# Batch 1's row maxima beside batch 0's scores: three banks, the free row groups, and an earlier place in the step

## What is computed

```python
scores = jnp.einsum('bshd,bthd->bhst', q, k) / jnp.sqrt(HEAD_DIM)
scores = jnp.where(causal, scores, -jnp.inf)
probs = jax.nn.softmax(scores, axis=-1)
out = jnp.einsum('bhst,bthd->bshd', probs, v)
```

## Time and profile before

| | us |
|---|---|
| median of 3 runs | 650.36 |
| the runs | 649.77, 650.36, 654.11 |
| profiled execution, its own time | 648.67 |
| its span, first to last instruction | 646.9 |
| layer 0's batch 0 attention, 92.65 to 159.59 | 66.94 |
| mean granted TensorE clock of the span | 0.811 |

### The profile page before, as it was taken

One profiled execution on the slowest core, in us unless ns is written; L12 is line 12 of the kernel. 1 busy time (PEld: TensorE's weight loads), 2 busy tenths in 40 slices (PEclk: granted clock), 3 DMA queues, 4 the chain that ended last, 5 costly groups with the idle time before them and its releaser, 6 DMA issues.

```text
span 646.9 us, 8796 instructions
## 1 busy us (share of the span) xinstructions
PE 467.8 (72%) x2581; PEld 296.1 (46%) x2581; DVE 341.4 (53%) x1150; ACT 234.8 (36%) x473; POOL 179.5 (28%) x275
## 2 busy tenths in 40 slices
PE   1876759888786377779376868676669999999410
PEld 1433334433442245326245524443348888886300
DVE  5376684555434672523536136149726766663545
ACT  2222134332554164544235645342033443430215
POOL 5111012211232031321002322111165555504751
PEclk9897765555987598986868877878599999999775
DMA  6000010000000000000000300499035555533332
GB/s 201 16 2 1 8 42 0 2 1 1 0 1 2 0 2 0 17 2 0 1 0 1 99 0 2 152 390 302 7 91 158 163 161 163 163 98 123 105 103 68
DMA packets 29766, 42.82 MB, mean 66 GB/s; under 512 B 3616, under 2 KB 21024, under 8 KB 29728
## 3 DMA queue, kind: packets, MB, share of 16 engines
q1 hardware_dynamic: 25120, 29.74, 13.5%
q0 software_dynamic: 4608, 12.59, 7.4%
HBM read 31.83 MB, written 10.49 MB: 65 GB/s over the span
## 4 chain that ended last, share of the span: by engine, by line
PE 55%; DVE 21%; ACT 8%; issue 7%; POOL 5%; another core or an unknown queue 2%; DMA 2%; SPq 0%; DVEq 0%; ACTq 0%; POOLq 0%
PE PSUM L657 10%; PE PSUM L957 8%; PE PSUM L601 5%; PE PSUM L630 5%; PE PSUM L947 4%; PE PSUM L782 3%; PE PSUM L671 3%; DVE st L1236 2%; POOL QP L583 2%; PE PSUM L938 2%; PE PSUM L607 2%; DVE H L1246 2%; PE PSUM L594 2%; PE PSUM L818 1%
## 5 line engine op out<-in xcount | busy, mean ns | idle before, releaser
L1047 ACT ACTIVATE PR<-PSUM 128x1024 f32<-128x1024 f32 (+1 forms) x96 | 82.1, 880 | 83.1 <-PE PSUM L671 82.8
L536 POOL TENSOR_SCALAR_AFFINE_SELECT PR<-PR 128x256 f32<-128x256 f32 x128 | 52.9, 428 | 177.1 <-ACT PR L1047 176.4
L1317 DVE CUSTOM_DVE_ANT_0 XN<-PSUM,XN 128x128 f32<-128x128 f32 (+3 forms) x128 | 58.1, 489 | 48.4 <-PE PSUM L630 48.1
L573 POOL DMA_INDIRECT QP<-tokens,tok_of x64 | 60.8, 950 | 56.1 <-PE PSUM L938 24.1
L657 PE MATMUL PSUM<-PR,VA 128*32 128x256 f32 (+3 forms) x512 | 60.1, 566 | 12.1 <-DVE XT L1366 9.7
L957 PE MATMUL PSUM<-arena,QP 128*128 x256 | 66.0, 380 | 3.5 <-ACT QP L1196 3.5
L671 PE MATMUL PSUM<-QT,KTr 32*128 32x384 f32 (+7 forms) x256 | 53.0, 450 | 12.8 <-ACT PR L1047 10.2
L630 PE MATMUL PSUM<-KTr,QT 32*128 32x128 f32 (+3 forms) x128 | 43.4, 536 | 14.6 <-DVE mx L1317 14.2
L957 PEld LDWEIGHTS PSUM<-arena,QP 128*128 128x128 f32 x256 | 48.2, 190 | 10.6 <-issue 4.2
L404 POOL TENSOR_TENSOR QP<-QK,QP 128x128 f32<-128x128 f32 (+1 forms) x16 | 9.5, 591 | 148.2 <-ACT QP L397 80.2
L601 PE MATMUL PSUM<-wq_sb,XT 128*128 128x512 f32 x64 | 40.7, 771 | 6.6 <-DVE QK L1298 4.0
(11 more groups left out here) (238 smaller groups left out, 821.9 us busy)
## 6 DMA issues: line engine op xcount, KB each, us to landing
arena<-in_wgu SPq DMA_DIRECT2D x4, 2048.0 KB, 15.7
expert_outputs<-QP SPq DMA_DIRECT2D x64, 128.0 KB
arena<-in_wd SPq DMA_DIRECT2D x2, 2048.0 KB, 16.6
wq_sb<-in_wqkv SPq DMA_DIRECT2D x2, 768.0 KB, 5.4
X<-in_x SPq DMA_DIRECT2D x2, 512.0 KB, 4.6
QP<-in_wsgu SPq DMA_DIRECT2D x1, 1024.0 KB, 5.4
tokens<-XN SPq DMA_DIRECT2D x2, 512.0 KB, 12.8
QP<-tokens,tok_of POOLq DMA_INDIRECT x64
```

Source lines behind the costliest of these rows:

```text
L536: ins = pool.affine_select(diag, diag, [[0, 2], [1, P]], ALU.is_ge, 0.0, base=0, channel_multiplier=-1)
L573: pool.indirect_dma_start(out=XG[:, i % U, :], out_offset=None, in_=h_dram, in_offset=bass.IndirectOffsetOnAxis(ap=tok_of[:, i:i + 1], axis=0)
L1047: did(sc.activation(PR[:, n % PSLOTS, 2 * half:2 * half + 2, 0:WIDTH[chunk]], PSUM[:, 2 * half:2 * half + 2, 0:WIDTH[chunk]], ACT.Exp, sca ...
L1317: did(dv.tensor_tensor_reduce(MSK[m % 2][:, 0:nk], o[:, 0:nk], MASKQ[:, S - nk:S], op0=ALU.add, op1=ALU.max, scale=1.0, scalar=NEG, accum_ ...
```

## The change

The 68 operations are laid out by step in a table. In step n two maxima of the wide tiles (tile 3, 512 keys, in steps 0 to 7; tile 2 in 8 to 15; tile 1 in 16 to 23) are taken from heads in the two row groups that the step's scores don't use. In every third step (2, 5, ..., 23) two maxima of tile 0, 128 keys, are added; these lie in the row groups of the scores. Turns come at steps 9, 17, 25 and 26, for tiles 3, 2, 1, 0. The operations use banks 5, 6 and 7 in turn, and operation k waits for the reading of operation k - 3. TensorE's order in a step of this stage becomes scores, beside, weighing. All quads of batch 0 are weighed in bank 4, so each weighing of a quad's first chunk waits for the copy of the quad before, and that copy is taken at step 9 of a quad in place of 10. Batch 1's quads keep banks 4 and 5.

```diff
-TURN_LATER, MAX_STEPS = 5, STEPS + 1
+MAX_BANKS = 3
+TURN_AT = ((9, 3), (17, 2), (25, 1), (26, 0))
+MAX_STEPS = 27
+def max_beside_ops():
+    ops, narrow = [], 0
+    for step in range(MAX_STEPS):
+        free = 2 - 2 * (step % 2)
+        if step < STEPS:
+            tile, n = TB - 1 - step // 8, step % 8
+            ops += [(step, "max", tile, 4 * (n // 2) + free + a) for a in range(2)]
+            if step % 3 == 2:
+                ops += [(step, "max", 0, 2 * narrow + a) for a in range(2)]
+                narrow += 1
+        ops += [(step, "turn", tile, None) for at, tile in TURN_AT if at == step]
+    return ops
...
+        def max_bank(k):
+            return bank(5 + k % MAX_BANKS)
+        def weigh_bank(b, q):
+            return bank(4 + q % 2 if b else 4)
...
# TensorE: weigh, attend, max_beside
-                if c >= 2 and chunk == 0:
-                    pe.wait_ge(s_pve, c - 1 + l)
+                if c and chunk == 0:
+                    pe.wait_ge(s_pve, c if l or c <= QUADS else c - 1)
...
-                                o, lhs = bank(4 + q % 2), VA[:, b * TB + j, m, :]
+                                o, lhs = weigh_bank(b, q), VA[:, b * TB + j, m, :]
...
+                    if beside is max_beside and step < steps:
+                        beside(step)
                     if weighs_at(step):
                         weigh(l, b, *weighs_at(step))
-                    if step < steps:
+                    if beside is not max_beside and step < steps:
                         beside(step)
...
-                for k, (kind, n) in max_ops(step):
-                    if k >= 2:
...
+                for k, kind, tile, head in max_ops(step):
+                    if k >= MAX_BANKS:
+                        if BESIDE[k - MAX_BANKS][1] == "max":
+                            pe.wait_ge(s_mrd, len(MUNITS) + MAX_NO[k - MAX_BANKS] + 1)
                         else:
-                            pe.wait_ge(s_rq, TB + before_n + 1)
+                            pe.wait_ge(s_rq, TB + TURN_NO[k - MAX_BANKS] + 1)
...
# VectorE: evacuate, attend
-                    did(dv.tensor_copy(OT[:, q, :], bank(4 + q % 2)), s_pve)
+                    did(dv.tensor_copy(OT[:, q, :], weigh_bank(b, q)), s_pve)
...
-                    if quad_at(step, TAKE_AT) is not None:
-                        evacuate(l, b, quad_at(step, TAKE_AT))
+                    take_at = TAKE_AT if l or b else SUM_AT
+                    if quad_at(step, take_at) is not None:
+                        evacuate(l, b, quad_at(step, take_at))
```

More of the change, by code:

```diff
@@ L49 @@
 TURNS = [(0, 0), (0, 1)] + [(k, b) for b in (0, 1) for k in (1, 2)] + [(3, 0), (3, 1)]
-TURN_LATER, MAX_STEPS = 5, STEPS + 1
+MAX_BANKS = 3
[13 more added lines that the diff above has]
+    return ops
+BESIDE = max_beside_ops()
+LAST_HEAD = {tile: max(k for k, op in enumerate(BESIDE) if op[1:3] == ("max", tile)) for tile in range(TB)}
+MAX_NO = [sum(op[1] == "max" for op in BESIDE[:k]) for k in range(len(BESIDE))]
+TURN_NO = [sum(op[1] == "turn" for op in BESIDE[:k]) for k in range(len(BESIDE))]
 OUT0, LN1, ADD1, NORM2, TURN1, INNER, EXPS, GATED, UP = 0, 6, 6, 11, 13, 17, 19, 22, 27
@@ L356, in build @@
         MUNITS = [(i, n) for i in range(TB) for n in range(HEADS0)]
[L357 to L360, removed]
         def max_ops(step):
-            return [(k, op) for k, op in enumerate(MAX_OPS) if k * (MAX_STEPS - 1) // (len(MAX_OPS) - 1) == step]
+            return [(k, kind, tile, head) for k, (at, kind, tile, head) in enumerate(BESIDE) if at == step]
+        def max_bank(k):
+            return bank(5 + k % MAX_BANKS)
+        def weigh_bank(b, q):
+            return bank(4 + q % 2 if b else 4)
         def turn_bank(c, n):
@@ L623, in turn_padded0, with maxima @@
                     mm.then_inc(s_tps, 1)
-            def maxima(b, m, o):
-                i, n = MUNITS[m]
+            def maxima(b, i, n, o):
                 g, row = slot(0, n)
@@ L631, in maxima, with turn_again @@
                           start=True, stop=True).then_inc(s_mps, 1)
-            def turn_again(b, i, o):
-                pe.wait_ge(s_neg, b * TB + i + 1)
+            def turn_again(b, i, o, no):
+                pe.wait_ge(s_neg, b * TB + no + 1)
                 for g in range(4):
@@ L851, in _ @@
                     pe.wait_ge(s_tev, 2 * turned + 1)
-                    turn_again(0, n, bank(6))
+                    turn_again(0, n, bank(6), n)
                     again = n + 1
@@ L863, in _ @@
                     for m in (2 * n, 2 * n + 1):
-                        maxima(0, m, bank(m % 4))
+                        maxima(0, *MUNITS[m], bank(m % 4))
             pe.wait_ge(s_tev, 2 * NT)
@@ L1066, in max_beside @@
             def max_beside(step):
-                for k, (kind, n) in max_ops(step):
+                for k, kind, tile, head in max_ops(step):
                     if kind == "turn":
-                        store_again(1, n, bank(6 + k % 2))
+                        store_again(1, tile, max_bank(k), TURN_NO[k])
             def after0(b, step):
@@ L1170, in _ @@
                 if kind == "again":
-                    store_again(0, n, bank(6))
+                    store_again(0, n, bank(6), n)
             sc.wait_ge(s_lamd, 1)
@@ L1308, in prepare0, with maxima @@
                 did(dv.tensor_tensor(ra, ra, rb, ALU.add), s_ro)
-            def maxima(b, m, o):
-                i, n = MUNITS[m]
+            def maxima(b, m, i, n, o, last_head):
                 nk, c = (i + 1) * P, b * TB + i
@@ L1380, in max_beside @@
             def max_beside(step):
-                for k, (kind, n) in max_ops(step):
+                for k, kind, tile, head in max_ops(step):
                     if kind == "max":
-                        maxima(1, n, bank(6 + k % 2))
+                        maxima(1, MAX_NO[k], tile, head, max_bank(k), k == LAST_HEAD[tile])
             def after0(b, step):
@@ L1527, in _ @@
                     for m in (2 * n, 2 * n + 1):
-                        maxima(0, m, bank(m % 4))
+                        maxima(0, m, *MUNITS[m], bank(m % 4), MUNITS[m][1] == HEADS0 - 1)
             dv.wait_ge(s_w0, 64)
```

13 lines of the change are left out of this document (5 added, 8 removed).

## The result

| | before | after |
|---|---|---|
| median, all runs of the first comparison (4 each) | 651.42 us | 628.69 us |
| lowest, highest | 649.77, 654.11 | 620.61, 638.27 |
| ratio after/before, 95% interval | | 0.954 [0.947, 0.961] |
| profiled execution, its span | 648.67, 646.9 | 623.23, 621.5 |

The ratio leaves out executions that are over 1.5% above the fastest of their kernel (634 and 638 us here); the medians of all runs differ by 22.7 us. The forecast was 633.4 us, a ratio of 0.974. Measured was a gain of 4.6%, nearly twice as much: set against 650.36 us it is 620.6, outside the range of 623 to 643. Repeated on two other chips, the same kernel gave 0.977 [0.969, 0.985] and 0.980 [0.975, 0.986], close to what had been forecast. This document is about both: why the stage came out near what was worked out, and what the first comparison had on top.

The account below looks back on a forecast made before the run. TensorE's program order, two banks handed between it and VectorE, was taken to bound the stage. Steps summed to 54.5 us at half clock, 49.5 with the clock's rise; 17 off gave 633.4 us, range 623 to 643.

Parts of the forecast that it names:

- The sum at half clock: Batch 0's layer 0 attention, all parts added at half clock: 54.5 us against 66.94, 12.4 us less.
- Step (b): Waits in the stage's steps: 1.0 to 1.3 us without weighing, 2.65 with weighing and two maxima; four-maxima steps wait anew.
- S: TensorE's time for two scores and two maxima together: some 0.78 us, bounds 0.42 and 1.2.
- Four row groups at once: Two maxima run beside each step's two scores, in some 0.78 us where the maxima alone take 0.79 each.
- The three-bank term: Loop over three banks in steps without weighing: half of (1.58 + 0.61), 1.10 us per step at 512 keys.
- The clock in the stage: Clock rises between steps 7 and 18, falling at times; half behind step 9 at full clock, stage 49.5 us, gain 17.4.
- a fuller array makes the clock rise: Being busy is not enough; steps 7 and 8 and turn-weighing pairs in 17, 25, 26 make fuller stretches.
- The two stretches that the forecast compared: TensorE at 157 to 160, clock 1.00 from 160.48, against 119.0 to 122.5, with fewer row groups in part, clock 0.50.
- cases A and B: A: clock low until the tail, gain 13, 637.4 us, chance 0.27. B: as forecast, 633.4 us, chance 0.45.
- Transposes and the clock: Turns help the clock rise, going by a profile row against the skill page; by the page, 12 to 13 us gain.
- if the stretches behind the stage change by more than 4 us: A sign that the forecast is wrong, beside a stage over 58 us or maxima starting 0.4 or more behind scores.
- Rival E: Slower: clock low behind the stage, in the next attention; 12.4 us won, up to 20 lost, 658 us; chance 0.06.

Follow-up runs that it names:

- the second profile: The changed kernel repeated unchanged, against the kernel before: stage 55.09 us at a mean clock of 0.51, ratio 0.977 [0.969, 0.985].

## Why the prediction was right, and where it was wrong

**The sum at half clock: right, partly by luck.** Forecast for the whole 54.5, set to half clock 55.6; by part 11.1, 13.6, 13.0 against 11.22, 13.46, 14.07, and 16.8 for the last two against 16.35 in the second profile, 1.0 us of it at full clock. Single steps were not right. Steps 6, 7 and 8 were worked out at 1.3, 2.65 and 2.8 us and took 0.60, 3.61 and 2.91 (from the starts of their first scores). Step (b), "in a weighing step with two maxima VectorE works under the weighing, so the step is S + 1.87", failed: the reduction of step 6's first maximum still ran, until 103.68, when step 7's second maximum wanted its bank (the 0.40 us at 103.82), ahead of the weighing. What the forecast charged to step 6 was paid in step 7, and the two together came out near the sum, 4.21 us against 3.95. That this error cancelled was luck: the forecast didn't see it.

**Four row groups at once: right.** Four matmuls in 0.69 us; with the row groups taken wrongly the stage grows by 3.3 us.

**The three-bank term, not separated in the forecast, is the largest.** At half clock the third bank takes 7.1 us off the kernel before and 8.4 off the change; the order is worth 1.5 alone and 3.4 in the change, the row groups 3.3 there. With two banks all the rest of the change brings 2.9 us. In a chain from before: the banks 7.1, then the table 0.8, then the order 3.4, 11.3 us in all; only the 7.1 is nearly free of the clock's price. The order's part needs the table's row groups, so the last two terms can't be told apart further.

**The clock in the stage: a rise, but later and not by the reason given.** It rose 39 to 40 us into the stage in two profiles, around steps 18 and 19, and in the tail in one; forecast was between steps 7 and 18. The reason was that a fuller array makes the clock rise, with steps 7 and 8 as the first such stretch. They came as described, and the clock stayed at 0.50 through them and through the whole second part, with TensorE busy for 12.56 of 13.46 us. The two stretches that the forecast compared differ in more than the row groups: TensorE was busy for 3.00 of 3.00 us in the one and for 3.27 of 3.50 in the other. So the stage took 51.4 to 55.1, between cases A and B, and 12 to 15.5 us were gained in place of 17. What makes the clock rise in it stays open.

**Transposes and the clock.** The Trainium skill, "TensorE: Matmul & The Clock Gate", Part 4 (PE-mode transpose), says that transposes do not count as busy the same way. The tail of the changed kernel doesn't decide it, as weighings stand between its turns. The earlier trace rows speak against the page, and in the changed kernel's profile the same turns do so again. Sixteen transposes start at 230.49, after TensorE was idle for 3.28 us:

```profile
230.49 3.34 PE L812 MATMUL PSUM<-ident,QP 128*128 128x128 f32 x16 [3.28 <-POOL QP L434]
```

The granted clock was 0.50 from 230.50 to 233.30, with nothing but these transposes on TensorE, and 1.00 from 233.50 to 236.70.

**The failed step: the sum took everything outside the stage as unchanged.** The 17 us of the stage were the whole forecast, and all other stretches stood in it at nothing, though it named as a sign of being wrong "if the stretches behind the stage change by more than 4 us". They did, both ways. In the profiled pair the stage gave 15.3 us and all the rest together 10.1: the opening 1.7, the loop 3.5, the end 9.6, by the late event that was missing, and the next attention took back 4.75. The change has no part in them as far as the runs show. In 14 further executions of the same kernel no run was under 633.0 us, and both repeated ratios hold the forecast 0.974 to within 0.6%. What the gain on record has beyond the forecast belongs to the first comparison, for the larger part to the missing late event (9.6 of the 10.1 us net). That the first chip or its state favours this kernel is not excluded; it wasn't tried on it again. The repeated ratios are near the forecast partly by luck as well: they hold a stage gain below 17 and a next attention that differs from run to run.

**Rival E in a mild form.** The next attention does cost time when its clock is low: 93.5 us at 0.81, 103.5 at 0.72, for the same work. But it isn't the change that lowers the clock, as before has 93.50 and 101.49 in its two profiles, nor the stage's length, as 102.93 and 95.24 stand behind stages of 54.80 and 55.09. What goes with it is where the clock's rise falls against the attention's first scores. It rises 0.7 us after them where it takes 93.50, 0.3 to 0.4 ahead in the three profiles with 101.44 to 101.49, 0.9 to 1.0 ahead in the two with 95.24 and 95.29, 2.2 ahead in the two with 102.92 and 102.93. A rise shifted by half a us to one us against the program goes with 6 to 8 us. It isn't the whole account: a rise 1.4 to 1.8 us ahead stands with 98.2 us in two profiles and with 103.5 in three.

**Open.** Why TensorE's semaphore comes late in the end, and why once it didn't. What sets the moment of the clock's rise ahead of the next attention; if the three to eight us that go there could be kept, the narrow maxima behind the weighing would be the version to use.

## What to carry to other kernels

When two engines hand PSUM banks back and forth, count the banks first: one more was worth more here (7.1 us) than the order and the row groups together (some 4), and with two banks all the rest brought 2.9. Small operations that wait for a bank did better here behind the long operation of their step, while the wide ones that have free row groups stood ahead of it. Before a difference of 3 us in a raw stage time is believed, the granted clock of the stage is to be read beside it, and that of the stages behind. And a first comparison that brings more than the changed stage can give is to be repeated and cut into stretches before the surplus is credited to the change.

## What was not expected of the hardware

TensorE ran 58.15 of 66.94 us at a granted clock of 0.50 without a rise, and in the changed kernel 34.7 of 38.75 us, though with four row groups in many steps. The same attention of the next batch took between 93.5 and 103.5 us in 14 profiles, in step with its mean clock of 0.81 to 0.72. And one wait of 10.3 to 11.1 us near the end stands in 13 of 14 profiles, whatever the kernel, on a semaphore that comes 8.1 to 9.9 us after the recorded end of the matmul that raises it.
